# Linear attention on one core: all attention-value products of a half ahead of its query-state products

## The reference, cut to what matters

```python
def step(S, inp):                      # one chunk of tokens after the other
    qi, ki, vi, bi = inp               # bi: running sum of g inside the chunk
    o_inter = einsum('bhtd,bhde->bhte', qi * exp(bi), S)
    ...
    A = einsum('bhtd,bhjd,bhtjd->bhtj', qi, ki, exp(diff))   # causal
    o_intra = einsum('bhtj,bhje->bhte', A, vi)
    ...
    S_new = exp(blast)[:, :, 0, :, None] * S + einsum('bhtd,bhte->bhde', kdec, vi)
    return (S_new, o_inter + o_intra)
...
o = o * rsqrt(mean(o * o, axis=-1, keepdims=True) + EPS) * rms_w
gate = silu(x @ Wg.T)
return o.reshape(B, N, DV) * gate @ Wout.T
```

## Time and profile before

| | |
|---|---|
| time, median of 3 runs | 1723.2 us (1719.59 to 1725.48) |
| the profiled execution | 1716.48 us |
| its span, first to last instruction | 1714.4 us |
| busy share of the span | TensorE (PE) 96%, VectorE (DVE) 67%, ScalarE (ACT) 50%, POOL 39% |
| mean granted TensorE clock | 0.989 |

### The profile page before, as it was taken

The page is one execution under the profiler, slowest core; times in us unless marked ns, Lnnn a source line. Parts: engine busy times, 40 slices in busy tenths (PEclk is TensorE's granted clock), DMA queues, the critical chain, the costliest instruction groups (busy, mean ns, idle before and its releaser), DMA issues.

```text
span 1714.4 us, 41995 instructions
## 1 busy us (share of the span) xinstructions
PE 1638.2 (96%) x14962; PEld 1106.0 (65%) x14963; DVE 1146.9 (67%) x2505; ACT 858.2 (50%) x1474; POOL 671.4 (39%) x652
## 2 busy tenths in 40 slices
PE   6999999999989999999999999999999989998999
PEld 3665656666567776765565656666566767777666
DVE  6677766666556666656766656666677678776675
ACT  4455434444466555644343334444466566564774
POOL 2342333444122222123342333444244488888243
PEclk9999999999999999999999999999999999998999
DMA  7132323333302111002210123333322033221011
GB/s 249 53 110 84 97 85 98 110 106 104 84 13 38 24 25 24 1 1 84 87 50 26 37 75 96 111 108 101 96 63 48 2 76 77 54 62 40 14 37 50
DMA packets 90149, 115.69 MB, mean 67 GB/s; under 512 B 9296, under 2 KB 76400, under 8 KB 90032
## 3 DMA queue, kind: packets, MB, share of 16 engines
q1 hardware_dynamic: 69680, 71.17, 14.8%
q0 software_dynamic: 20352, 42.88, 8.8%
HBM read 66.11 MB, written 47.90 MB: 67 GB/s over the span
## 4 chain that ended last, share of the span: by engine, by line
PE 81%; DVE 7%; POOL 4%; ACT 4%; issue 3%; DMA 2%; SPq 0%; DVEq 0%; ACTq 0%; POOLq 0%
PE ps L1701 18%; PE ps L1703 18%; PE ps L1702 18%; PE ps L1944 3%; PE ps L1945 3%; PE ps L1717 3%; PE ps L2042 2%; PE ps L1925 2%; PE ps L1926 2%; PE ps L1863 2%; PE ps L1882 2%; PE ps L2199 2%; PE ps L2181 1%; PE ps L2169 1%; PE ps L2047 1%
## 5 line engine op out<-in xcount | busy, mean ns | idle before, releaser
L719 POOL DMA_INDIRECT routed<-work x142 | 136.5, 961 | 234.5 <-DVE work L1456 229.4
L1701 PE MATMUL ps<-later_hi,work 128*128 (+1 forms) x632 | 203.0, 321 | 1.2 <-ACT work L1054 1.0
L1702 PE MATMUL ps<-later_lo,work 128*128 (+1 forms) x632 | 203.0, 321 | 0.0
L1703 PE MATMUL ps<-later_hi,work 128*128 (+1 forms) x632 | 202.9, 321 | 0.0
L1701 PE MATMUL ps<-xt_hi,wsh 128*128 128x512 f16 x512 | 195.1, 381 | 5.3 <-DVE work L1344 3.0
L1702 PE MATMUL ps<-xt_lo,wsh 128*128 128x512 f16 x512 | 195.0, 381 | 0.0
L1703 PE MATMUL ps<-xt_hi,wsh 128*128 128x512 f16 x512 | 194.9, 381 | 0.0
L864 ACT ACTIVATE work<-ps 128x512 f32<-128x512 f32 x128 | 76.4, 597 | 182.4 <-PE ps L1703 182.1
L650 POOL TENSOR_TENSOR rstd<-mv,eps 128x4 f32<-128x4 f32 x49 | 14.7, 300 | 385.9 <-DVE mv L1149 375.1
L1701 PE MATMUL ps<-wsh,work 128*128 128x256 f16 x512 | 140.3, 274 | 4.0 <-ACT work L853 2.7
L1703 PE MATMUL ps<-wsh,work 128*128 128x256 f16 x512 | 140.4, 274 | 0.0
(11 more groups left out here) (247 smaller groups left out, 4234.2 us busy)
## 6 DMA issues: line engine op xcount, KB each, us to landing
work<-expert_x SPq DMA_DIRECT2D x142, 129.0 KB, 2.1
yg<-in_w_later SPq DMA_DIRECT2D x9, 496.0 KB, 3.5
w1q<-in_w_later SPq DMA_DIRECT2D x9, 496.0 KB, 3.7
yg<-in_w SPq DMA_DIRECT2D x8, 512.0 KB, 3.6
values<-wsh SPq DMA_DIRECT2D x8, 512.0 KB, 3.3
later_hi<-values SPq DMA_DIRECT2D x16, 256.0 KB, 4.6
later_lo<-values SPq DMA_DIRECT2D x16, 256.0 KB, 4.7
out_x<-x SPq DMA_DIRECT2D x8, 512.0 KB, 3.0
```

The source lines that it names most:

```text
L719: nc.gpsimd.indirect_dma_start(routed[:, :], bass.IndirectOffsetOnAxis(m.homes[:, i:i + 1], 0), m.t_y[:, i % 4, :], None).then_inc(s[f"til ...
L1701: nc.tensor.matmul(out_, a[0], b[0], start=start, stop=False)
L1702: nc.tensor.matmul(out_, a[0], b[1], start=False, stop=False)
L1703: return nc.tensor.matmul(out_, a[1], b[0], start=False, stop=stop)
```

## The change

The loop over blocks becomes a loop over halves j. Within a half, first all eight products of attention and values are issued, then those of queries and states. The first product that is issued into a bank carries the start flag (which clears the bank's accumulation state); the others of that bank don't, and the last one carries the stop flag. Before, every block and pair had its own start and stop. The waits for the mask stay at the head of a half; those for the states stand ahead of the block's query-state products instead of ahead of the whole block.

```diff
-                    for c in range(TPS):
-                        if c % 2 == 0:
-                            pe.wait_ge(s["masked"], g * 2 + c // 2 + 1)
-                        if c:
+                    for j in range(2):
+                        pe.wait_ge(s["masked"], g * 2 + j + 1)
+                        for c in range(2 * j, 2 * j + 2):
+                            for p in range(GPAIR):
+                                for h in range(2):
+                                    own = slice((2 * p + h) * DV, (2 * p + h + 1) * DV)
+                                    nc.tensor.matmul(ps[:, 2 * j + h, block(c, h, p)], m.att[:, j, h, c % 2, p], m.v[:, c, own],
+                                                     start=c == 2 * j and p == 0, stop=False, skip_group_check=True)
+                        for c in range(max(2 * j, 1), 2 * j + 2):
                             pe.wait_ge(s["s_step"], g * 5 + 2 * c - 1)
-                        for p in range(GPAIR):
-                            for h in range(2):
-                                ins = nc.tensor.matmul(ps[:, c // 2 * 2 + h, block(c, h, p)], m.att[:, c // 2, h, c % 2, p],
-                                                       m.v[:, c, (2 * p + h) * DV:(2 * p + h + 1) * DV], start=True, stop=c == 0)
-                            if c:
+                            for p in range(GPAIR):
                                 for h in range(2):
                                     rows_ = slice(h * DK, (h + 1) * DK)
-                                    ins = nc.tensor.matmul(ps[:, c // 2 * 2 + h, block(c, h, p)], m.q[rows_, p, c * P:(c + 1) * P],
-                                                           m.states[rows_, c - 1, p], start=False, stop=True)
-                        if c % 2:
-                            ins.then_inc(s["o_ready"], 1)
+                                    ins = nc.tensor.matmul(ps[:, 2 * j + h, block(c, h, p)], m.q[rows_, p, c * P:(c + 1) * P],
+                                                           m.states[rows_, c - 1, p], start=False,
+                                                           stop=c == 2 * j + 1 and p == GPAIR - 1, skip_group_check=True)
+                        ins.then_inc(s["o_ready"], 1)
```

## The result

| | before | after |
|---|---|---|
| median of 6 runs | 1724.34 us (1719.47 to 1728.33) | 1712.01 us (1708.79 to 1714.43) |
| ratio | | **0.9927**, 95% interval 0.9912 to 0.9943 |
| span of the profiled execution | 1714.4 us | 1709.9 us |
| output products of one sequence, all eight alike | 7.28 us | 5.70 us |

The change makes the kernel 12.3 us faster; 12.6 us were forecast. The interval alone leaves 9.8 to 15.2 us; that the gain is 1.57 us in each sequence is seen in the trace. A second set of six runs on another occasion gave 0.9929 (0.9908 to 0.9949).

The account below looks back on a forecast made before the run. TensorE's own queue was taken to bound the linear attention stage. Eight sequences at 1.57 us less gave 12.6 us, taken from a median of 1723.2 us: 1710.6 us forecast, range 1704 to 1717.

Parts of the forecast that it names:

- Step 1: TensorE's output products: four runs instead of twelve, eight switches gone at 0.19 to 0.20 us, 1.57 us less per sequence.
- Step 2: Attention-value products on TensorE: runs of 16 rows keep the pace of 12, about 0.112 us a row.
- Rival D: Long attention-value runs lose their pace, 0.21 us a row from unhidden weight loads: 9.2 us slower, 1732.4 us; chance 0.02.
- Steps 4 and 5: TensorE's mask and state waits are all met, costing nothing; ScalarE's squares and query copies come earlier or unchanged, delaying nothing.
- Step 6: VectorE's decay through POOL's scaling to the turning stays put; slack falls from 1.1 to 0.5 us, TensorE still doesn't wait.
- Rival B: The VectorE and POOL chain before the turning becomes the wait: 5.6 us lost over seven sequences, 1716.2 us; chance 0.07.
- The clock: TensorE's half clock, about 38 us of the span, may shift the time 4 us either way; chance of more 0.04.

Follow-up runs that it names:

- x1: Kernel before, product order kept, only the change's flags (one start and one stop per bank): ratio 0.9999, output products 7.28 us a sequence.
- x2: The change's flags, but products grouped by block instead of by half, six runs: ratio 0.9950 to the kernel before, output products 6.10 us a sequence.
- x4: Order of the kernel before, the change's flags, query-state products on all 128 rows (computes something else): output products 6.36 us a sequence.
- x3: The change, but all attention-value products of both halves first, then all query-state products: ratio 0.9915 to the kernel before, output products 5.31 us a sequence.
- x7: x3 with VectorE's residual and statistics put ahead of the decay: ratio 0.9902 to the kernel before, 36.90 us between middle sequences.
- x6: The change plus one needless power on POOL ahead of each sequence's root: distances 37.30 us, but 37.81, 37.82 and 37.90 in three sequences.
- x5: The change with head as outer and pair as inner loop in the query-state products of each block: output products 5.81 us a sequence.
- x10: The change with the head loop outside the blocks of a half in the query-state products: output products 6.26 us a sequence.
- x11: x3 with the head loop outside everything, twelve query-state rows of one array half before twelve of the other: output products 6.30 us a sequence.

## Why the prediction was right

- **Step 1, the sum.** 1.57 us a sequence, in all eight; 12.6 us forecast, 12.3 us measured, 1712.0 us where 1710.6 stood. x1, x2 and x4 show that its cause is the one named: the number of runs sets it (0.197 us each, twelve, six, four and two runs), the flags don't, and without a change of shape there is no pause.
- **Step 2, the pace of long runs.** 16 rows go at the pace of 12, and 32 in x3 as well: 3.77 us to the next run, 0.112 a row. Rival D is out: loads of 192 ns start every 112 ns in one row group, as the earlier trace rows showed. The rule that the forecast cites from the Trainium skill ("TensorE: Matmul & The Clock Gate", Part 3, "The mechanism"), that loads overlap only when the row group differs, doesn't hold here. An earlier sentence of that section, which also lets a load for the background weight buffer be pulled ahead, fits these rows; I had left it out. The Trainium skill ("TensorEngine Tiling (Array Packing)", "Key Properties") says that a change of the tiling mode drains the engine. The traces fit it: going from 128 to 64 rows of the array or back costs 0.197 us, and x4, without such a change, has no pause. That a drain fills those 0.197 us, no row shows.
- **Steps 4 and 5, waits and followers.** No wait came in. In the long-chain sequences ScalarE's second square follows its first without a gap (one row, x2). In the ones between them it still waits, but starts 5.82 instead of 7.39 us behind the first output product, 1.57 earlier. The query copies follow TensorE's projections, 1.57 us earlier too:

```profile
614.53 1.92 ACT L986 ACTIVATE work<-ps 128x1024 f32<-128x1024 f32 x2
...
617.90 0.60 ACT L965 ACTIVATE work<-ps 128x512 f32<-128x512 f32 x1 [0.70 <-PE ps L1703]
```

- **Step 6, the chain that does not move.** Its course was right, its slack was not. It was put at 0.5 us and is 0.2:

```profile
621.80 2.94 POOL L736 TENSOR_TENSOR work<-work,neghalf 128x16 f32<-128x16 f32 x1
624.82 4.12 POOL L741 TENSOR_TENSOR work<-work 128x1024 f32<-128x1024 f32 x2
...
624.11 1.22 DVE L1542 TENSOR_TENSOR work<-work 128x1024 f32<-128x1024 f32 x1
627.12 1.22 DVE L1592 TENSOR_TENSOR work<-work,ps 128x1024 f32<-128x1024 f32 x1 [1.79 <-POOL work L741]
...
628.55 1.04 PE L2066 MATMUL ps<-consts,work 128*128 128x128 f32 x8
```

  The scaling was taken at 1.88 us a half, as the earlier trace rows had it. It now starts 0.5 us before VectorE's product of keys and decays (L1542) ends, and both halves take 4.12 instead of 3.76 us. Rival B spoke of this overlap, and I dismissed it because the 1.88 us looked "the same in the rows whether VectorE works or waits". In the sequence of the earlier trace rows the two overlap by only 0.06 us. The first sequence of the kernel before has an overlap of 0.4 us, and its scaling takes 4.01 us. I hadn't looked there (POOL, then VectorE):

```profile
509.06 4.01 POOL L741 TENSOR_TENSOR work<-work 128x1024 f32<-128x1024 f32 x2 [2.40 <-ACT work L993]
508.24 1.22 DVE L1542 TENSOR_TENSOR work<-work 128x1024 f32<-128x1024 f32 x1
```

  The longer scaling cost nothing in the change, since 0.2 us were left. In x3 it alone, 0.37 us, is more than the 0.30 lost. In the long-chain sequences the two instructions overlap by less than 0.1 us in x7 and not at all in x6, and both halves take 3.75.
- **Rival B's price.** It was put on seven sequences. x3 and x6 lost time in the three with the long chain only; the other four have 0.85 to 1.1 us of slack after the change.
- **The clock.** The mean granted clock was 0.989 before and 0.991 after. By the forecast's own sum the lower level (1.2 GHz) then holds for 2 x 0.009 x 1710 = 31 us instead of 38, which is worth at most 3.5 us, within the 4 us that the range allowed.

## What to carry to other kernels

Read TensorE's timeline by starts, not by busy time: it was "busy" for 99% of a sequence, and changes of shape took a third of the output products' time (12 x 0.197 of 7.28 us). Products that use a part of the array's rows belong together, and so do those that use all of them; what each change between them costs can be read as the intercept of run length over rows, and a grouping be summed before it is written. When TensorE's part gets shorter, look for the chain that does not move with it and for what it will newly overlap: here its slack fell from 1.1 to 0.2 us, and the next 0.4 us saved hit it. And read all sequences of a stage, not one: the first one of the kernel before already showed what that overlap costs.

## What the runs showed that I had not expected

- Rows of the two halves of the array don't start in the order of the program: an upper row passes up to three lower ones (x5, x10, x11). So the inner order of two heads costs 0.1 us at four rows of each in turn, 0.55 us at eight.
- Full-row products without any partner, but without a change of shape (x4, 6.36 us; it computes something else), beat paired half-row products in the order of before (7.28 us). Grouping beats both (5.70 us).
- A product of VectorE with two inputs in SBUF and POOL's scaling get in each other's way: an overlap of 0.5 us made POOL's two instructions 0.37 us longer (4.12 against 3.75). The Trainium skill ("SBUF — State Buffer", "Who interferes with whom") says that a VectorE instruction with two inputs in SBUF contends with a GpSimd instruction that reads SBUF, and that the later one is blocked until the first is through. The traces of before, after and x3 agree. VectorE's product keeps its 1.22 us. The first scaling, 1.90 us when it is undisturbed, takes 1.92 us at an overlap of 0.16 us, 1.99 at 0.24, 2.15 at 0.39 and 2.27 at 0.51: from 0.16 us on it ends 1.76 us behind VectorE's product each time. Each further 0.1 us of overlap costs 0.1 us, as with blocking; evenly shared ports would cost half of that (an estimate).
